# Fourteen fp32 down products of a macaron block's second FFN pass, split into fp32r high and low parts

## What is computed

```python
g = jnp.einsum('nh,ehm->enm', x, w_gate)
u = jnp.einsum('nh,ehm->enm', x, w_up)
inter = jax.nn.silu(g) * u
y_e = jnp.einsum('enm,emh->enh', inter, w_down)
y = jnp.einsum('ne,enh->nh', combine, y_e)
shared = jnp.dot(jax.nn.silu(jnp.dot(x, sw_gate)) * jnp.dot(x, sw_up), sw_down)
...
x = x + 0.5 * _L0_ffn_ref(_layernorm(x, axis=-1), ...)
x = x + _L0_attn_ref(_layernorm(x, axis=-1), ...)
x = x + 0.5 * _L0_ffn_ref(_layernorm(x, axis=-1), ...)
```

## Time and profile before

| | us |
|---|---|
| median of 3 runs | 293.48 (291.27 to 295.85) |
| the profiled execution | 292.86 |
| span of its trace | 291.1 |
| PE busy | 269.6 (93%) |
| DVE busy | 187.0 (64%) |
| ACT busy | 150.7 (52%) |
| POOL busy | 120.4 (41%) |

### The profile page before, as it was taken

How to read it: one execution, slowest core, us unless ns; L and a number is a source line. 1 busy time by engine, 2 the same in 40 slices (tenths; PEclk the granted TensorE clock), 3 DMA queues, 4 the chain that set the end, 5 groups by cost and what they waited for, 6 DMA issues and landing times.

```text
span 291.1 us, 4514 instructions
## 1 busy us (share of the span) xinstructions
PE 269.6 (93%) x1316; PEld 175.7 (60%) x1316; DVE 187.0 (64%) x564; ACT 150.7 (52%) x281; POOL 120.4 (41%) x108
## 2 busy tenths in 40 slices
PE   8998989999999997899899489998999999999995
PEld 3676846565677653466566266466666666766661
DVE  4778964987654357767588267844695796694231
ACT  4775456345234512786677557786635725633320
POOL 5600096942999066350401200005323724680760
PEclk9999999999999999999999689999999999999999
DMA  6800895694439596476667812107100801801911
GB/s 191 268 5 7 252 179 149 207 147 134 160 97 313 120 199 158 83 186 145 133 180 157 136 34 60 31 7 244 45 3 24 268 0 42 269 22 42 286 40 36
DMA packets 44689, 36.82 MB, mean 127 GB/s; under 512 B 19744, under 2 KB 33144, under 8 KB 44664
## 3 DMA queue, kind: packets, MB, share of 16 engines
q1 hardware_dynamic: 43384, 36.39, 48.2%
q10 hardware_dynamic: 1280, 0.13, 0.4%
HBM read 31.71 MB, written 4.84 MB: 126 GB/s over the span
## 4 chain that ended last, share of the span: by engine, by line
PE 45%; DVE 16%; DMA 15%; issue 10%; ACT 7%; POOL 3%; SPq 3%; DVEq 0%; ACTq 0%; POOLq 0%
PE pY L1023 12%; DMA c_all<-comb_dram 4%; DMA q_t<-max_t 4%; PE pU L1094 3%; DVE neg_max L824 3%; PE pG L943 3%; PE pG L1079 3%; PE pU L943 3%; PE pU L945 3%; PE pU L944 3%; POOL ring L473 3%; PE pG L945 3%; PE pG L944 3%; DMA k_diag<-k_dram 2%; PE pY L1107 2%
## 5 line engine op out<-in xcount | busy, mean ns | idle before, releaser
L473 POOL TENSOR_TENSOR ring<-ring,c_all 128x512 f32<-128x512 f32 x57 | 71.9, 1287 | 48.3 <-DMA c_all<-comb_dram 42.4
L787 DVE TENSOR_TENSOR ring<-ring,pU 128x512 f32<-128x512 f32 x64 | 43.6, 683 | 39.6 <-PE pU L945 27.6
L548 ACT ACTIVATE ring<-pG 128x512 f32<-128x512 f32 x64 | 37.9, 597 | 57.3 <-PE pG L945 56.9
L1023 PE MATMUL pY<-ring,wd_sb 128*128 128x512 f32 x128 | 64.7, 598 | 1.2 <-POOL ring L473 1.1
L943 PE MATMUL pG<-xt_hi,wg_hi 128*128 128x512 f32 x72 | 46.1, 640 | 1.9 <-ACT ring L548 1.9
L584 ACT ACTIVATE probs<-pU 128x512 f32<-128x512 f32 x64 | 34.8, 596 | 15.5 <-PE pU L1094 14.2
L458 POOL TENSOR_TENSOR rstd<-var_eps,half 128x4 f32<-128x4 f32 x8 | 8.1, 1011 | 77.6 <-DVE var_eps L691 77.6
L824 DVE TENSOR_REDUCE neg_max<-pG 128x8 fp32r<-128x768 f32 x32 | 30.6, 956 | 12.7 <-PE pG L1079 12.5
L1023 PEld LDWEIGHTS pY<-ring,wd_sb 128*128 128x128 f32 x128 | 22.6, 189 | 11.2 <-issue 6.3
L943 PE MATMUL pU<-xt_hi,wu_hi 128*128 128x512 f32 x72 | 28.8, 400 | 0.4 <-DVE ring L787 0.2
L945 PE MATMUL pG<-xt_lo,wg_hi 128*128 128x512 f32 x72 | 28.4, 395 | 0.0
(11 more groups left out here) (135 smaller groups left out, 439.8 us busy)
## 6 DMA issues: line engine op xcount, KB each, us to landing
c_all<-comb_dram SPq DMA_DIRECT2D x64, 256.0 KB, 4.4
q_stage<-q_dram SPq DMA_DIRECT2D x16, 192.0 KB
q_t<-q_dram SPq DMA_DIRECT2D x16, 192.0 KB
k_diag<-k_dram SPq DMA_DIRECT2D x32, 72.0 KB
q_dram<-q_hi SPq DMA_DIRECT2D x8, 256.0 KB, 3.9
X<-x SPq DMA_DIRECT2D x4, 256.0 KB, 3.9
q_t<-qrows_dram SPq DMA_DIRECT2D x2, 512.0 KB
q_dram<-q_lo SPq DMA_DIRECT2D x4, 256.0 KB, 4.2
```

The lines of the kernel that those rows point to most:

```text
L473: pool.tensor_tensor(ring_at(n), ring_at(n), c_all[:, n % CH], ALU.mult)\
L548: act.activation(ring_at(n), pG[:, n % 2], ACT.Silu).then_inc(silu_done, 1)
L787: dve.tensor_tensor(ring_at(n), ring_at(n), pU[:, n % 2], ALU.mult).then_inc(gu_done, 1)
L1023: pe.matmul(pY[:, u % 2], wd_sb[:, D * e:D * (e + 1)], ring_at(n), start=e == 0, stop=e == CH - 1)\
```

## The change

For 14 of the 36 chunks of pass two (m = 5, 6, 7, then 14, 15, 16, then 23 to 26 and 28 to 31) `down` becomes three fp32r products, of a high and a low part of both operands, as gate and up are computed already. ACT makes the high part of the weights (`wd_hi`, three copies of 128x384 in slots ATTN 18 to 20) and of each hidden tile (`hid_hi`, 128x512, in slot m+4, ahead of that slot's silu). POOL makes the low part of the weights (three subtractions of 128x384 in ATTN 19, ATTN 20 and slot 3), DVE that of each hidden tile (`hid_lo`, in slot m+4, ahead of that slot's gu). The new tiles lie in `k_diag`. The tables of slots for everything else are as before.

```diff
--- before.py
+++ after.py
@@ -47,6 +47,10 @@
...
+SPLIT_LAG = 4
+SPLIT = [PASS + n for n in (5, 6, 7, 14, 15, 16, 23, 24, 25, 26, 28, 29, 30, 31)]
@@ -91,6 +95,9 @@
...
+DOWN_HI = {(ATTN, 18): 0, (ATTN, 19): 1, (ATTN, 20): 2}
+DOWN_LO = {(ATTN, 19): 0, (ATTN, 20): 1, (FFN2, 3): 2}
...
@@ -207,6 +214,12 @@
...
+        k_diag_flat = k_diag[:].rearrange("p h b j k -> p (h b j k)")
+        wd_hi, wd_lo = (k_diag_flat[:, i * CH * D:(i + 1) * CH * D] for i in range(2))
+        hid_hi, hid_lo = ([k_diag_flat[:, 2 * CH * D + (2 * i + j) * SEQ:2 * CH * D + (2 * i + j + 1) * SEQ]
+                           for j in range(2)] for i in range(2))
...
@@ -473,6 +488,11 @@
...
+            def down_weights_lo(i):
+                pool.wait_ge(wd_hi_done, i + 1)
+                pool.tensor_tensor(third(wd_lo, i), third(wd_sb, i), third(wd_hi, i).bitcast(F32), ALU.subtract)\
+                    .then_inc(wd_lo_done, 1)
...
@@ -551,6 +573,21 @@
...
+            def down_weights_hi(i):
+                act.wait_ge(wd_in[i], 16)
+                act.wait_ge(s_psum, 2 * NG)
+                act.activation(third(wd_hi, i), third(wd_sb, i), ACT.Copy).then_inc(wd_hi_done, 1)
+
+            def hid_high(n):
+                i = SPLIT.index(n)
+                if n % CH < NP2:
+                    act.wait_ge(hid_done, hids(n))
+                else:
+                    act.wait_ge(gu_done, n + 1)
+                if i >= 2:
+                    act.wait_ge(down_done, SPLIT[i - 2] + 1)
+                act.activation(hid_hi[i % 2], ring_at(n), ACT.Copy).then_inc(hid_hi_done, 1)
...
@@ -627,8 +664,13 @@
...
+                for n in chunks(kind, t, SPLIT_LAG):
+                    if n in SPLIT:
+                        hid_high(n)
                 for n in chunks(kind, t, 0):
                     silu(n)
+                if slot in DOWN_HI:
+                    down_weights_hi(DOWN_HI[slot])
...
@@ -786,6 +828,12 @@
...
+            def hid_low(n):
+                i = SPLIT.index(n)
+                dve.wait_ge(hid_hi_done, i + 1)
+                dve.tensor_tensor(hid_lo[i % 2], ring_at(n), hid_hi[i % 2].bitcast(F32), ALU.subtract)\
+                    .then_inc(hid_lo_done, 1)
...
@@ -885,6 +933,9 @@
...
+                for n in chunks(kind, t, SPLIT_LAG):
+                    if n in SPLIT:
+                        hid_low(n)
                 for n in chunks(kind, t, 0):
                     gu(n)
...
@@ -1016,6 +1067,17 @@
...
+                if n in SPLIT:
+                    i = SPLIT.index(n)
+                    if i == 0:
+                        pe.wait_ge(wd_lo_done, 3)
+                    pe.wait_ge(hid_lo_done, i + 1)
+                    pe.matmul(pY[:, u % 2], wd_hi[:, cols], hid_hi[i % 2], start=e == 0, stop=False)
+                    pe.matmul(pY[:, u % 2], wd_lo[:, cols], hid_hi[i % 2], start=False, stop=False)
+                    pe.matmul(pY[:, u % 2], wd_hi[:, cols], hid_lo[i % 2], start=False, stop=e == CH - 1)\
+                        .then_inc(down_done, 1)
+                    return
...
```

More of the change, by code:

```diff
@@ L246, in macaron @@
         hid_done, down_done = sem("hid_done"), sem("down_done")
+        wd_hi_done, wd_lo_done, hid_hi_done, hid_lo_done = (
+            sem(n) for n in ("wd_hi_done", "wd_lo_done", "hid_hi_done", "hid_lo_done"))
         y_copied, y_back, x_added = sem("y_copied"), sem("y_back"), sem("x_added")
@@ L510, in _ @@
                     add_bias(BIAS[slot])
+                if slot in DOWN_LO:
+                    down_weights_lo(DOWN_LO[slot])
                 if slot in Q_SPREAD:
@@ L1018, in down @@
                         pe.wait_ge(o_norm_done, NG)
+                cols = slice(D * e, D * (e + 1))
+                if n in SPLIT:
[8 more added lines that the diff above has]
+                    return
                 if e < NP2:
```

## The result

The changed kernel takes 293.91 us (median of 22 runs, 291.52 to 295.88), the kernel before 292.48 us (22 runs beside them); the ratio of the two is 1.0074, with a 95% interval of 1.005 to 1.0099. The ratio and its interval leave out the slow executions, which the median of 292.48 still has in it. So it is slower by some 2.2 us (0.74% of 292.5), where I forecast it faster by 0.4. The profiled execution has a span of 293.0 us and a mean granted clock of 0.981, against 291.1 and 0.988 before.

What follows compares the result with a forecast made beforehand. PE was taken to set the end in slots 19 to 35, with DVE's routing handing back earlier gains. +1.24 - 0.3 - 1.36 = -0.4 us gave 292.4 from the profiled execution, 293.1 from the median; stated 292.8 us, range 290.7 to 295.0.

Steps and rivals of the forecast that it cites:

- The gain of one product: Each changed down on PE: three fp32r products at 0.23 us replace one of 0.86, 0.17 us shorter, 2.4 us for 14.
- Group one, +1.24: Chunks 5 to 7: ACT's copy waits for hid(6) ahead of normalize; logits 1.24 us late, no gain kept.
- my upper bound of 1.6: Chunks 5 to 7: logits at most 1.6 us late, if POOL's hid(7) holds up chunk 6's subtraction.
- such a fall: A granted clock that falls in attention, among the unseen causes for which 0.05 was left; no size given.
- Groups three and four, -1.36: Chunks 23 to 26 and 28 to 31: nothing is short, so eight products gain 0.17 us each, 1.36 us together.
- POOL "hardly gives": POOL's operation stays at 1.25 to 1.38 us in all 57 cases, also when DVE works beside it.
- Group two, -0.3: Chunks 14 to 16: PE waits 0.2 us for xt_lo at logits, gaining 0.14, plus 0.17 with chunk 16: 0.3 us shorter.
- The weighed case that two subtractions stand in front of xt_lo: Chunks 14 to 16: two DVE subtractions precede xt_lo; if POOL holds up each, logits come 1.1 us late; chance 0.2.
- Of the rivals, the second: POOL and DVE hold each other up at chunks 14 to 16: +0.8 us in sum, 293.7 us, slower; chance 0.2.
- The weights were rightly costed at nothing: Three weight copies on ACT and subtractions on POOL, in the first stretch: no cost, or 0.1 to 0.2 us if cover fails.

Runs made afterwards that it cites:

- pe_kept_busy: The changed kernel plus seven unused fp32r products on PE in slot 11, ahead of the transposes: 292.58 us, ratio 1.0041 to the kernel before.
- chunk_six: The changed kernel with only chunk 6 split instead of fourteen chunks: 293.47 us, ratio 1.0081 to the kernel before.
- copy_behind_normalize: The changed kernel with chunk 6's high copy behind silu and normalize in slot 10, its subtraction behind gu: 293.43 us, ratio 1.0057 to the kernel before.
- full_again: The changed kernel, text unchanged, run and traced a second time: 295.15 us beside 293.35 for the kernel before, one run each.
- group_one: The changed kernel with only chunks 5, 6 and 7 split: 293.89 us beside 291.96, ratio 1.0057 to the kernel before.
- no_group_one: The changed kernel with chunks 5, 6 and 7 left in fp32 and the other eleven split: 292.33 us, ratio 1.0008 to the kernel before.

## Why the prediction was wrong

I forecast -0.4 us; the pass is 97.36 - 95.24 = 2.12 us longer, and 0.83 us longer where the clock held (pe_kept_busy). By its steps:

- **The gain of one product**: right. Three fp32r products at 0.23 us take the place of 0.86, the slots of group three are 2.08 us long, and the stretch gives 0.64 us for four.
- **Group one, +1.24**: the mechanism was right, the list of what it triggers was not complete. chunk_six shows the queue of ACT behind hid(6) alone, 0.97 us at the transposes, and copy_behind_normalize takes it away again. At g22 the group costs 1.13 at full clock, near the forecast, though at the logits it is 1.66, beyond my upper bound of 1.6, with a power that is 0.37 longer beside DVE's subtraction, which I had left out because no row of before has POOL as a loser. The Trainium skill (SBUF — State Buffer, Who interferes with whom) says that of two such instructions the loser is blocked; the trace agrees, with POOL as the loser here.
- **The step that failed first** is the one that isn't there: a wait of 2 us on PE was priced at its own length. Behind it the granted clock fell to 0.50 and cost 1.0 us more (logits at 34.95 against 33.95, g22 at 60.03 against 59.05 with the gap filled), and 1.36 at g22 in full_again. The prediction gave such a fall 0.05, and in attention, not here. What decides whether it falls behind the same wait is open: in group_one it held.
- **Groups three and four, -1.36 ("Nothing is short here")**: the second failed step. Group three gave 0.64 and group four, behind it, nothing in the changed kernel (14.21 us from g32 to the end where it was 14.20), and between -0.15 and 0.28 in the five other traces that split both with the high part in SBUF, instead of 0.68. I had checked chunk 28, with a subtraction held up once, and wrote that the later chunks have as much. They have less: each step of the chain POOL, ACT, DVE is slower than I took it, and PE's own gain in group three is what runs it into that chain. That POOL "hardly gives" was read from a trace in which no 128x512 product or subtraction of DVE has both its operands in SBUF; beside such a one it does, with 11.9 instead of 10.1 us for eight.
- **Group two, -0.3**: not shown. no_group_one is 0.13 us ahead at g22, within the spread of 0.42, so these traces can't size it; in the changed kernel PE waits 0.3 us for xt_lo, where I had put 0.2. The weighed case that two subtractions stand in front of xt_lo was right, not its size.
- **The routing between groups two and three**: no step spoke of it. From g22 to g28 the seven kernels that change nothing earlier take 13.90 to 14.09 us, the seven others 14.24 to 14.37. The loss is at gate(24) to gate(26), 5.38 us in the changed kernel and 4.93 before: up starts 0.35 us behind the product ahead of it, not 0.23, at both gates, because a gu stands behind the routing on DVE. (The 0.2 us of PE pU L994 in the list above is another place, slot 15, at 234.14; so is that of the earlier trace rows, at 231.73, which I took for up(19); the sum doesn't use it.) The routing's steps r_den and r_choice together take 0.49 us in the trace of before, where POOL pauses at r_choice, and 1.38 to 1.63 in these seven, where POOL multiplies beside them; the six others of the first kind have 1.13 to 1.40, so this is a part of the loss and not the whole. Rows of before and of chunk_six:

```profile
251.48 0.29 DVE L733 TENSOR_TENSOR r_choice<-r_score,gbias_sb 128x128 f32<-128x128 f32 x1
252.59 1.33 DVE L775 TENSOR_TENSOR r_choice<-r_score,gbias_sb 128x128 f32<-128x128 f32 x1
```

Why a split ahead of slot 22 shifts POOL against the routing is open; a late pass isn't needed for it, as no_group_one is not late at g22 and loses the same.

Together, at full clock: +1.13 (group one), +0.2 (group two; 59.05 against 58.84, within the spread), +0.4 (routing; 14.33 against 13.92), -0.9 (groups three and four; 22.69 from g28 to the end against 23.61) make the 0.83 us of pe_kept_busy. The clock's 1.0 and 0.3 in the later stretches, mostly group four, make it 2.12. Of the rivals, the second came nearest, slower through DVE and POOL, but not at its place: I put it in group two, and it showed in group four, in the routing and, by the power, in group one. That its 293.7 us lies next to the measured 293.91 is luck, since its sum has no clock in it. The weights were rightly costed at nothing.

## What to carry to other kernels

A step that is cheap by itself is priced by what stands behind it in its engine's queue: splitting one chunk, with one 0.63 us copy ahead of normalize, cost 0.79 us at the logits and 1.25 at the end (chunk_six), half of all that fourteen shorter products could give. When two gains follow each other on the bound engine, the second must be checked at the time at which PE arrives with the first one in hand, against producers that start by a DMA's landing and don't move. And where VectorE gets new work with two operands in SBUF beside GpSimd, charge both engines for it. One operand in PSUM freed both engines here, but the copy that put it there cost ScalarE 0.60 us a tile, and no trace shows that the pass gained by it.

## What the runs showed of the hardware

- A wait of 2.0 us on TensorE, in a stretch in which it was otherwise busy, was followed by a granted clock of 0.50 in two of three traces, for about 3 us in one and over 6 in the other, and products 0.43 us apart instead of 0.23; in group_one, after the same wait, it held, as it did in the one trace each after 1.4 us, after 1.1 us and with the gap filled.
- GpSimd and VectorE held each other up where both read two operands from SBUF: 1.48 against 1.26 us an operation on GpSimd (up to 1.82), 0.90 to 1.80 against 0.69 us on VectorE, and GpSimd's 128x4 power 1.38 against 1.01 us. With one of VectorE's operands in PSUM neither lost anything (10.03 us for eight of GpSimd's, 0.69 us for each of VectorE's).
